# Two-layer attention and experts kernel: key chunks of equal width and bursts of three slots, PSUM banks grouped otherwise, and the row maxima carried to the query rows by DMA

## What is computed

```
x = x + tanh(g_xattn[0]) * attention0(layernorm(x), context)     # 16 heads of 8, 1024 x 6404 scores each
x = x + tanh(g_ffn[0])   * experts0(layernorm(x))                # 8 experts, top 2, gelu
x = x + tanh(g_xattn[1]) * attention1(layernorm(x), context)     # with a mask, here all ones
x = x + tanh(g_ffn[1])   * experts1(layernorm(x))                # 8 experts, top 2, silu

attention: softmax(q k^T / sqrt(8)) v, head by head, then the output projection
```

## Time and profile before

| what | us |
|---|---|
| median of three runs | 2560.41 |
| lowest and highest of them | 2549.94 and 2565.13 |
| span of the profiled execution, first to last instruction | 2547.9 |
| busy in it: TensorE, VectorE, ScalarE | 2478.7, 2113.7, 1936.6 |

### The profile page before, as it was taken

The page is one execution under the profiler, slowest core; times in us unless marked ns, Lnnn a source line. Parts: engine busy times, 40 slices in busy tenths (PEclk is TensorE's granted clock), DMA queues, the critical chain, the costliest instruction groups (busy, mean ns, idle before and its releaser), DMA issues.

```text
span 2547.9 us, 50971 instructions
## 1 busy us (share of the span) xinstructions
PE 2478.7 (97%) x21057; PEld 944.1 (37%) x21057; DVE 2113.7 (83%) x2093; ACT 1936.6 (76%) x3561; POOL 86.2 (3%) x89
## 2 busy tenths in 40 slices
PE   9999999999999999997988999999999999999989
PEld 4433333333333333333443333333333333333343
DVE  6799999999999999724358999999999999999044
ACT  4388888888888888873321888888888888888921
POOL 4200000000000000001000000000000000000000
PEclk8799999999999999997985999999999999999989
DMA  4311111111110000021001000000000000000000
GB/s 172 114 38 40 39 40 40 39 40 39 40 40 31 29 29 30 6 101 53 4 24 50 20 30 30 30 30 30 30 30 30 30 30 30 30 30 9 2 1 9
DMA packets 38323, 93.53 MB, mean 37 GB/s; under 512 B 5604, under 2 KB 17032, under 8 KB 37832
## 3 DMA queue, kind: packets, MB, share of 16 engines
q1 hardware_dynamic: 36568, 89.87, 10.1%
q10 hardware_dynamic: 1520, 0.37, 0.1%
HBM read 73.18 MB, written 15.74 MB: 35 GB/s over the span
## 4 chain that ended last, share of the span: by engine, by line
PE 92%; DVE 6%; DMA 1%; ACT 1%; issue 0%; ACTq 0%; POOL 0%; DVEq 0%; POOLq 0%
PE ps L1177 34%; PE ps L1133 28%; PE ps L1158 15%; DVE m_part L846 5%; PE ps L1292 4%; PE ps L1300 3%; PE ps L1089 1%; PE ps L1057 1%; PE ps L1190 1%; PE ps L1123 1%; PE ps L1312 1%; DMA w_att<-in_wq 0%; ACT probs L666 0%; PE ps L1268 0%; PE ps L1098 0%
## 5 line engine op out<-in xcount | busy, mean ns | idle before, releaser
L846 DVE TENSOR_REDUCE m_part<-ps 128x2 f32<-128x1024 f32 (+1 forms) x1664 | 1944.2, 1185 | 131.3 <-PE ps L1158 115.2
L666 ACT ACTIVATE probs<-ps 128x512 f32<-128x512 f32 (+1 forms) x3264 | 1761.4, 595 | 273.3 <-PE ps L1133 159.0
L1177 PE MATMUL ps<-probs,v_all 128*9 128x256 f32 x13056 | 1010.8, 381 | 1.5 <-ACT o_raw L646 0.3
L1133 PE MATMUL ps<-q_ring,k_ring 35*128 35x512 f32 x3264 | 866.0, 497 | 0.3
L1158 PE MATMUL ps<-k_ring,q_ring 33*128 33x512 f32 (+1 forms) x3328 | 718.6, 409 | 25.6 <-DVE m_part L846 22.7
L1133 PEld LDWEIGHTS ps<-q_ring,k_ring 35*128 35x128 f32 x3264 | 344.5, 183 | 708.4 <-ACT probs L666 622.3
L1177 PEld LDWEIGHTS ps<-probs,v_all 128*9 128x9 f32 x13056 | 194.2, 88 | 572.6 <-ACT probs L666 503.3
L1158 PEld LDWEIGHTS ps<-k_ring,q_ring 33*128 33x128 f32 x3328 | 347.0, 191 | 89.5 <-DVE m_part L846 74.8
L620 ACT ACTIVATE v_all<-ps 128x512 f32<-128x512 f32 (+1 forms) x26 | 15.2, 584 | 86.1 <-PE ps L1089 86.1
L719 ACT ACTIVATE probs<-ps,b_col 128x512 f32<-128x512 f32 x32 | 20.2, 683 | 66.9 <-PE ps L1292 66.9
L876 DVE RECIPROCAL den_t<-den_t 128x256 f32<-128x256 f32 x2 | 3.5, 1753 | 78.2 <-DMA o_t<-o_raw 78.2
(11 more groups left out here) (145 smaller groups left out, 641.6 us busy)
## 6 DMA issues: line engine op xcount, KB each, us to landing
k_ring<-k_parts SPq DMA_DIRECT2D x372, 96.0 KB
k_ring<-k_parts SPq DMA_DIRECT2D x124, 112.2 KB
big<-in_mask_t SPq DMA_DIRECT2D x10, 640.0 KB, 11.8
k_parts<-k_ring SPq DMA_DIRECT2D x12, 512.0 KB, 3.1
k_parts<-big SPq DMA_DIRECT2D x12, 512.0 KB, 3.1
q_ring<-q_parts SPq DMA_DIRECT2D x120, 32.0 KB
big<-in_w SPq DMA_DIRECT2D x1, 2048.0 KB, 9.5
ctx_t<-in_w SPq DMA_DIRECT2D x1, 2048.0 KB, 9.4
```

Source lines behind the costliest of these rows:

```text
L666: A(probs[0:k, n % PSLOTS, HALF * half:HALF * half + HALF], ps[0:k, e_bank(unit), :], ACT.Exp, scale=SCALE).then_inc(sem(f"exp_done{l}"), 1)
L846: V.tensor_reduce(m_part[:, h % 2, :, p, c], mx(n % 2)[:, :, 0:chunk_w[c]], AX.X, ALU.max).then_inc(sem(f"mx_done{l}"), 1)
L1133: pe.matmul(bank, k_ring[row:row + ROWS_EXP, koff:koff + P], q_ring[row:row + ROWS_EXP, qoff:qoff + HALF], start=not masked, stop=True).th ...
L1177: mm = pe.matmul(ps[32 * g:32 * g + VW, 7, 0:QGW], v_all[:, t, h, :], probs[:, n % PSLOTS, QGW * g:QGW * g + QGW], start=(t == 0), stop=(t ...
```

## The change

- **Equal chunks.** The 13 key chunks of the maximum pass are all 494 wide (`MXW`); the last begins at key 5910 and overlaps the one ahead of it. There are still 104 half units a head.
- **Bursts.** The 51 slots become 34 bursts of three scores. A burst issues S, M, S, M, S, M (each M a half unit of 494 columns, alternating the rows of the array), then V of the burst ahead: one whole slot (4 matmuls of 256 columns) and half a slot (4 of 128 columns). Bursts 9 and 21 have a fourth M. Query halves swap their order at those places (`first_half`). Bank 7 holds V as 4 groups of 2 x 128.
- **Reductions.** The four banks are used one by one. VectorE reduces two banks in one instruction where the burst's banks allow it, and one otherwise (`reductions`): of four bursts in turn, three have a pair and a single, and one has three singles.
- **The maximum by DMA.** For heads 1 to 15 `whole_max` writes `m_rows`, and `place_rows` on SP's queue issues 16 DMAs (2 halves, 2 parts, 4 groups) that each carry one value of 128 partitions into 128 neighbouring elements of one row of `q_ring`. The first S of a head waits for all 16. The rows unit on TensorE and ScalarE's two copies stay for head 0 alone.
- **Warming.** `dense`: 8 groups of `keep_warm` in burst 0 and 5 in bursts 1 to 5 of head 0, and 2 in the last two bursts of every head. Before: 4 in each of the first two slots of head 0 and 3 in each of the next 8.
- Semaphores are shared between layers, and `normalise` reads the new order of bank 7.

```diff
+QB = HALF // QG
+BURST = 3
+BURSTS = 2 * NT // BURST
-def dense(l, h, t):
-    return 3 if h == 0 and t < 8 else 0
+def dense(l, h, b):
+    if b >= BURSTS - 2:
+        return 2
+    return (0 if h else 8 if b == 0 else 5 if b < 6 else 0)
+MXW = 494
+MX_BANKS = 4
+MORE_AT = (9, 21)
+def max_from(c):
+    return min(MXW * c, TK - MXW)
+def first_half(t):
+    return 1 - sum(t >= BURST * (b + 1) // 2 for b in MORE_AT) % 2
+def fills(h, b):
+    n, end = 2 * LOOP_AT[h], 2 * LOOP_AT[h + 1]
+    first = n + BURST * b + sum(at < b for at in MORE_AT)
+    return range(min(first, end), min(first + BURST + (b in MORE_AT), end))
+def reductions():
+    at = [(2 * n, 2) for n in range(len(FIRST_UNITS))]
+    for h in range(H):
+        for b in range(BURSTS):
+            halves = fills(h, b)
+            m = halves.start
+            while m < halves.stop:
+                alone = m % MX_BANKS == MX_BANKS - 1 or len(halves) == BURST and halves.start % MX_BANKS == MX_BANKS - 1
+                n = 2 if m + 1 < halves.stop and UNITS[m // 2][1] == UNITS[(m + 1) // 2][1] and not alone else 1
+                at.append((m, n))
+                m += n
+    return at
...
+            def place_rows(l, h):
+                off = h % QRING * HALF
+                sp.wait_ge(sem(f"m_low{l}"), h + 1)
+                for half in range(2):
+                    for part in range(2):
+                        row = HB * half + KR + 1 + part
+                        for p in range(NPAIR):
+                            sp.dma_start(q_ring[row:row + 1, off + P * p:off + P * p + P].bitcast(F32),
+                                         m_rows[:, part, p, half:half + 1].bitcast(F32)).then_inc(rows_in(l, h)[0], 16)
...
                         load_keys(l, h, g)
+                        if g == len(K_GROUPS) - 2:
+                            place_rows(l, h - KRING + 1)
...
-                dve.wait_ge(sem(f"mx_filled{l}"), n + 1)
-                V.tensor_reduce(m_part[:, h % 2, :, p, c], mx(n % 2)[:, :, 0:chunk_w[c]], AX.X, ALU.max
+                dve.wait_ge(sem(f"mx_filled{l}"), m + n)
+                V.tensor_reduce(parts[:, bank:bank + n, at], ps[:, bank:bank + n, 0:MXW], AX.X, ALU.max
                                 ).then_inc(sem(f"mx_done{l}"), 1)
...
+                if u == 0 and h:
+                    pe.wait_ge(*rows_in(l, h))
...
+                if m >= MX_BANKS:
+                    pe.wait_ge(sem(f"mx_done{l}"), REDUCED_AT[m - MX_BANKS] + 1)
...
+            def weigh_burst(l, n):
+                if n % 2:
+                    weigh(l, n // 2, 1, 1)
+                    weigh(l, n // 2 + 1, 0, 2)
                 else:
+                    weigh(l, n // 2, 0, 2)
+                    weigh(l, n // 2 + 1, 0, 1)
...
+                    for b in range(BURSTS):
+                        halves = fills(h, b)
+                        for i, unit in enumerate(burst_scores(h, b)):
                             score(l, unit, masked)
+                            if i < len(halves):
+                                max_half(l, halves[i], masked)
+                        for m in halves[BURST:]:
+                            max_half(l, m, masked)
...
+                        n = BURST * (h * BURSTS + b - 1)
                         if n >= 0:
+                            weigh_burst(l, n)
+                        for _ in range(dense(l, h, b)):
+                            keep_warm()
```

More of the change, by code:

```diff
@@ L94, in max_units, with burst_scores @@
     seq += [("max", h + 2, j) for j in range(AHEAD)] if h + 2 < H else []
[L95 to L98, removed]
+    return seq
 FIRST_UNITS = [("max", 0, j) for j in range(NU)] + [("max", 1, j) for j in range(AHEAD)]
-UNITS = FIRST_UNITS + [u for h in range(H) for step in max_units(h) for u in step]
+UNITS = FIRST_UNITS + [u for h in range(H) for u in max_units(h)]
 UNIT_AT = {u: n for n, u in enumerate(UNITS)}
[L106 to L114, removed]
+LOOP_AT = [len(FIRST_UNITS) + sum(len(max_units(i)) for i in range(h)) for h in range(H + 1)]
+MX_BANKS = 4
[20 more added lines that the diff above has]
+    return at
+REDUCTIONS = reductions()
+REDUCED_AT = {m + i: n for n, (m, count) in enumerate(REDUCTIONS) for i in range(count)}
+def burst_scores(h, b):
+    return [("score", h, BURST * b + i) for i in range(BURST)]
+SCORES = [("rows", 0, 0)] + [u for h in range(H) for b in range(BURSTS) for u in burst_scores(h, b)]
 SCORE_AT = {u: n for n, u in enumerate(SCORES)}
@@ L262, in move_rows @@
             if what < QG:
-                eng.dma_start(o_t[HD * h:HD * h + HD, QGW * what:QGW * what + QGW], o_raw[32 * what:32 * what + HD, :]
+                eng.dma_start(o_t[HD * h:HD * h + HD, :].rearrange("p (a g q) -> p a g q", a=2, g=QG)[:, :, what, :],
+                              o_raw[32 * what:32 * what + HD, :].rearrange("p (a q) -> p a q", a=2)
                               ).then_inc(sem("o_moved"), 16)
@@ L660, in exp_unit @@
                 _, h, u = unit
-                t, half = u // 2, u % 2
+                t, half = u // 2, (u + first_half(u // 2)) % 2
                 k, n = width(t), h * NT + t
-                if half == 0 and n >= PSLOTS:
+                if u % 2 == 0 and n >= PSLOTS:
                     act.wait_ge(sem(f"pv_done{l}"), n - PSLOTS + 1)
@@ L672, in exp_all @@
                 for h in range(H):
[L673 to L679, removed]
+                    for b in range(BURSTS):
+                        for unit in burst_scores(h, b):
+                            exp_unit(l, unit)
+                        if h and b == 0:
                             evacuate(l, h - 1)
@@ L864, in maxima @@
                 dve.wait_ge(sem("constants"), 1)
-                for n, (_, h, j) in enumerate(UNITS):
-                    max_tile(l, n, h, j)
-                    if j == NU - 1:
+                for m, n in REDUCTIONS:
+                    reduce_halves(l, m, n)
+                    _, h, j = UNITS[(m + n - 1) // 2]
+                    if j == NU - 1 and (m + n) % 2 == 0:
                         whole_max(l, h)
@@ new lines, in weigh @@
+            def weigh(l, n, first, count):
+                h, t = n // NT, n % NT
+                last = first + count - 1
+                low, high = sorted((first_half(t) ^ first, first_half(t) ^ last))
+                if t == 0 and h and count == 2:
+                    pe.wait_ge(sem(f"o_raw{l}"), h)
+                pe.wait_ge(sem(f"exp_done{l}"), SCORE_AT["score", h, 2 * t + last] + 1)
+                of = probs[:, n % PSLOTS, :].rearrange("p (a g q) -> p a g q", a=2, g=QG)
+                for g in range(QG):
+                    mm = pe.matmul(ps[32 * g:32 * g + VW, 7, QB * low:QB * high + QB], v_all[:, t, h, :],
+                                   of[:, low:high + 1, g, :], start=(t == 0), stop=(t == NT - 1 and last == 1),
+                                   skip_group_check=True)
+                if last == 1:
+                    mm.then_inc(sem(f"pv_done{l}"), 1)
```

148 lines of the change are left out of this document (69 added, 79 removed).

## The result

The kernel after takes 3655.95 us (median of 4 runs, 3654.15 to 3658.17) where the kernel before, timed beside it, takes 2556.84 (4 runs, 2549.94 to 2565.13): 1.429 times as long, with a 95% interval of 1.425 to 1.433. The forecast was 2525, its range 2465 to 2612.

A forecast was written before the change was run, and what follows sets the result against it. TensorE was taken to set the pace. Fifteen heads a layer at 63.4 us for 64.35, set by the row DMAs, give -28.5 us and the last heads -6.6: in all -35, 2525 us, range 2465 to 2612.

The forecast's parts named there:

- The burst: TensorE in the heads' loop: a burst takes 1.80 us where 1.5 slots were 1.86.
- TensorE's head: 34 bursts, two fourth M and four warm groups: 62.3 us by TensorE alone, 2.0 under 64.35.
- rival 4: VectorE becomes the bound at 66.3 us a head, no single overlapping the next instruction: +52, 2612 us; chance 0.08.
- The landing: Row DMAs into `q_ring`: the last lands 2.1 us after its issue.
- rival 3: Row DMAs run one after another, element by element: 33.6 us, a head of 87.4, +685, 3245 us; chance 0.06.
- Rivals 5 and 6: TensorE's burst: pairs hide weight loads, 1.56 us, 2330 in all (chance 0.04); or no shorter burst, 2.02, +155, 2715 (0.04).
- the issue: SP issues the 16 row DMAs every 0.50 us, range 0.40 to 0.675, so the rows are in at 63.4 us.
- rival 2: Row DMAs issued every 0.675 us, rows late, in at 66.0 us: +43, 2603 us; chance 0.18.
- TensorE waits about 1 us at each head's start: First S of a head waits for the row DMAs, in at 63.4 us against TensorE's 62.3; 30 times.
- my list of what would make me wrong: Issue outside 0.40 to 0.675, landing not near 2, TensorE waiting more for VectorE than rows, clock falling at heads' starts.
- the moves out of `o_raw`, for which nobody waits until a head later: SP's queue: these moves stand behind `place_rows`, taken as harmless there.
- the last heads: Last head of each layer, without M: a burst of 1.53 us against 1.63, -6.6 us for both layers.

The follow-up runs named there:

- AHEAD = 12: The kernel after with 12 units of maxima running ahead instead of 8; 2524.74 us, 0.989 times before.
- the fastest version: The kernel after with AHEAD = 12 and head 13's moves out of `o_raw` queued ahead of the last head's 16 row DMAs; 2492.7 us, 0.976 times before.
- slots: The kernel before with a wait for small DMAs (2 in layer 0, 4 in layer 1) put in at head 4's start; 3587.2 us.

## Why the prediction was wrong

**What held.** The burst is 1.80 us as forecast (median 1.77). TensorE's head is 61.65 for 62.3, so the saving of 2 us a head is real: 2.7. VectorE has the 2406 reductions, pairs of 1.19 and singles of 0.66, and hides but for some 0.3 us a head (TensorE waits 8.1 us for it in the 30 heads with `AHEAD = 12`; behind `whole_max` a maximum starts 0.6 us late); rival 4 is wrong. The landing is 2.0 us for 2.1, and issues overlap their landings: rival 3's 33.6 us is wrong. Rivals 5 and 6 are wrong by the burst. DMA packets of the kernel after while the first 16 row DMAs run, 178.9 to 192:

```profile
DMA packets 2308, 0.05 MB, mean 4 GB/s; under 512 B 2304, under 2 KB 2304, under 8 KB 2306
```

2304 small packets are 144 for each of the 16 DMAs of 128 values. So the trace agrees with one descriptor per element, which the prediction took from the Trainium skill ("DMA: Bandwidth & Descriptors", Rules for kernel authors). What failed is rival 3's step from there, that the transfers would run one after another. Which DMA engines they used, no row here tells.

**The sum's first failing term, small: the issue.** I took 0.50 us an issue; at the first wait the 16 took 11.13 us, with starts 0.70 apart on average, over the upper bound of 0.675. Over the 30 heads of the kernel after this average is 0.64 to 0.70 (median 0.67), so the bound was right for a typical head. Group and landing of the DMAs in the kernel after:

```profile
q_ring<-m_rows SPq DMA_DIRECT2D x480, 0.5 KB, 2.0
```

The nearest row in kind (0.675, SBUF to SBUF) was the right one, and the nearest in shape (0.40 and 0.52, from DRAM) the wrong one. With 0.70 the rows are in at 53.8 + 15 x 0.70 + 2.0 = 66.3 instead of 63.4, and the wait is 4 us instead of 1. By itself that is rival 2, worth 2 us a head.

**The step that failed: "TensorE waits about 1 us at each head's start", priced at 1 us.** The sum charged a wait of TensorE with its length. I had the clock in hand: the earlier trace rows show 1.00 with 0.54 us of idle time in 257, rival 3 named a lost clock, and so did my list of what would make me wrong. But I gave it only to idle times of 24 us and put no price on it for 1 or 2. The heads of before could not show that price, as they have next to no idle time. But the same trace has both a fall behind short waits and rows at 0.50, where the units ahead of layer 1's slots run. Timeline of TensorE in before, one row at either clock, and a window:

```profile
1320.54 0.50 PE L1158 MATMUL ps<-k_ring,q_ring 33*128 33x512 f32 x2 [1.16 <-DVE m_part L846]
...
1388.13 0.79 PE L1158 MATMUL ps<-k_ring,q_ring 33*128 33x512 f32 x2
```

```profile
1340.00:1380.00 40.00, 30.01 (x93) 14.93 (x92) 34.89 (x32) 2.34 (x5) 0.00 (x0) 0.50 0.06 12
```

TensorE waited 1.16 us there and twice 0.63 right behind it, the clock fell at 1324.3 and came back at 1392.6, among dense matmuls. I took no such row; with one, or with the bound that a slot or burst costs up to twice as much at half the clock, the wait could have been priced. From the measured heads, one lost clock costs (102.3 - 61.65) x 15 = 610 us a layer at the most. And the forecast's 30 waits could not happen: behind the first the head is so long that the rows are in time.

The Trainium skill ("TensorE: Matmul & The Clock Gate", its table on why this matters for your kernels) asks that TensorE not idle for more than about 3 us between bursts. That would have flagged the 3.97 us here, and not the forecast 1 us. The traces agree with it on the long waits and differ on the short ones: those of 1.10 us (twice in two) and 1.32 us (once in two) lost the clock as well, and the measurement decides.

**A second step, hidden by the first:** "the moves out of `o_raw`, for which nobody waits until a head later". At the end of a layer they are issued a head late, behind the last 16 issues, and with `AHEAD = 12` the copy waited 1.16 us for them. I had listed the queue and not followed it to its last turn.

**And a small one:** the last heads. I forecast a burst of 1.53 us and -3.3 a head, from layer 1's 55.4 us for both the earlier trace rows. In the fastest version layer 1's is 57.1 us, and layer 0's is 67.5 where it was 67.7 (1079.86 to 1147.52): no gain in either.

## What to carry to other kernels

Before a change lets TensorE wait where it never did, ask what the clock does behind the wait, and price the loop at half the clock until something restores it; a wait of 1.32 us cost 498 here. Then choose in this order: make the producer earlier (one constant here, worth 1131 us), look for what stands ahead of it or behind it in its queue (one moved line, 32 us), and put warming behind a wait that must stay. A loop that is "97% busy" at full clock may be one that merely never lost it: a single wait put in on purpose tells.

## What the runs showed of the hardware

- Both loops run on at 1.00 and, once slow, at 0.50. At 0.50 TensorE is recorded busy 100% of the time for 1200 us and more and stays at 0.50 (slots: 386 to 1580). Without added warming the profiled runs have ten such stretches of over 700 us. Not one ended while maxima were running; seven ended in the last bursts of head 14 or in head 15, which have none (the kernel after did at 1613.1), and three lasted to the end of the layer's heads, all in layer 1.
- The same wait of 1.3 us lost the clock in one layer and not in the other. With the rows over TensorE and no added warming, a maximum 0.6 us late behind a busy VectorE stood close ahead of a fall in 2 of the 31 heads run at the full clock; in the other 29 the clock held past it. Row waits of up to 1.9 us behind 45 groups of warming never did.
- Five groups of `keep_warm` (20 matmuls of 256 bf16 columns) in each of five bursts brought the clock back within 7 to 14 us, 30 times in 30.
- DMAs of one column of 128 values to one row, SBUF to SBUF, 16 in a row: SP issued one every 0.67 us (median over 30 heads of the kernel after), each moved in 144 packets, and they landed 1.9 to 3.0 us after issue, median 2.0.
